# Row maxima of causal attention: rounded, split and turned by 32x32 blocks on VectorE and carried by DMA, instead of turned by TensorE and copied by ScalarE

## The reference

```python
xn = layernorm(x)
q, k, v = split(xn @ qkv_w + qkv_b, 3)          # 32 heads, D = 16
q, k = rope(q), rope(k)
scores = einsum('bqhd,bkhd->bhqk', q, k) / sqrt(D)
probs = softmax(scores + (1 - tril) * MASK_VAL)
ctx = einsum('bhqk,bkhd->bqhd', probs, v)
x = x + (ctx @ out_w + out_b) * silu(ffn(xn))
```

## Time and profile before

| | |
|---|---|
| median of 3 runs | 611.6 us (611.2 to 612.4) |
| the profiled execution's own time | 611.91 us |
| its span, first to last instruction | 610.0 us |
| TensorE busy | 590.7 us, 97% |
| VectorE busy | 383.0 us, 63% |
| ScalarE busy | 290.2 us, 48% |
| GpSimd busy | 386.2 us, 63% |
| granted TensorE clock | full in all of the span |

### The profile page before, as it was taken

One profiled execution on the slowest core, in us unless ns is written; L12 is line 12 of the kernel. 1 busy time (PEld: TensorE's weight loads), 2 busy tenths in 40 slices (PEclk: granted clock), 3 DMA queues, 4 the chain that ended last, 5 costly groups with the idle time before them and its releaser, 6 DMA issues.

```text
span 610.0 us, 9847 instructions
## 1 busy us (share of the span) xinstructions
PE 590.7 (97%) x3368; PEld 424.7 (70%) x3368; DVE 383.0 (63%) x912; ACT 290.2 (48%) x448; POOL 386.2 (63%) x598
## 2 busy tenths in 40 slices
PE   6999999999999999999999999999999999999996
PEld 5876666666677887666666666788887676767664
DVE  5986778666427489877786663366985261516257
ACT  3625777556734622276766566354122453232432
POOL 6896956656435578878575555348979594821363
PEclk9999999999999999999999999999999999999999
DMA  9788776654512237658577554942600000000002
GB/s 302 236 303 251 208 212 189 195 139 103 145 54 87 87 103 220 210 165 250 148 216 223 154 160 130 353 157 95 238 5 1 1 0 2 0 1 1 0 30 109
DMA packets 60369, 83.63 MB, mean 137 GB/s; under 512 B 17936, under 2 KB 26768, under 8 KB 60320
## 3 DMA queue, kind: packets, MB, share of 16 engines
q1 hardware_dynamic: 57968, 75.02, 41.2%
q10 hardware_dynamic: 2352, 8.00, 3.4%
HBM read 65.17 MB, written 26.99 MB: 151 GB/s over the span
## 4 chain that ended last, share of the span: by engine, by line
PE 79%; DMA 5%; DVE 3%; issue 3%; POOL 3%; ACT 3%; SPq 2%; POOLq 0%; ACTq 0%; DVEq 0%
PE proj_ps L1004 9%; PE proj_ps L1006 7%; PE proj_ps L1005 7%; PE ctx_ps L1161 5%; PE score_ps L1034 4%; PE proj_ps L1209 4%; PE proj_ps L1210 3%; PE scoreT_ps L1043 3%; PE score_ps L1004 2%; PE score_ps L1006 2%; PE score_ps L1005 2%; PE scoreT_ps L1004 2%; PE scoreT_ps L1006 2%; PE scoreT_ps L1005 2%; PE ctx_ps L1209 2%
## 5 line engine op out<-in xcount | busy, mean ns | idle before, releaser
L821 POOL TENSOR_TENSOR w_lo<-raw,w_hi 128x512 fp32r<-128x512 f32 x98 | 132.3, 1355 | 64.7 <-ACT w_hi L1374 59.2
L1555 DVE CUSTOM_DVE_ANT_0 score_ps<-score_ps,causal 128x512 f32<-128x512 f32 (+3 forms) x256 | 118.9, 522 | 60.7 <-PE score_ps L1034 60.5
L1423 ACT ACTIVATE probs_T<-scoreT_ps 128x1024 f32<-128x1024 f32 x80 | 82.2, 1027 | 46.1 <-PE scoreT_ps L1043 45.0
L1004 PE MATMUL proj_ps<-xn_hi,w_hi 128*128 128x512 f32 x224 | 96.8, 432 | 1.6 <-ACT by_sin L1352 1.2
L1006 PE MATMUL proj_ps<-xn_lo,w_hi 128*128 128x512 f32 x224 | 88.5, 395 | 0.0
L1005 PE MATMUL proj_ps<-xn_hi,w_lo 128*128 128x512 f32 x224 | 88.5, 395 | 0.0
L852 POOL TENSOR_SCALAR_AFFINE_SELECT probs_T<-probs_T 128x256 f32<-128x256 f32 x128 | 55.5, 457 | 14.2 <-ACT probs_T L1423 14.1
L1004 PEld LDWEIGHTS proj_ps<-xn_hi,w_hi 128*128 128x128 f32 x224 | 42.0, 188 | 26.6 <-issue 14.4
L1333 ACT ACTIVATE q_st<-one_turn_ps 2x512 fp32r<-2x512 f32 x64 | 37.5, 587 | 32.5 <-PE one_turn_ps L1020 32.1
L979 POOL TENSOR_TENSOR hsL<-hidden_T,hsH 128x256 fp32r<-128x256 f32 x44 | 37.6, 872 | 23.4 <-ACT hsH L1495 22.9
L1006 PEld LDWEIGHTS proj_ps<-xn_lo,w_hi 128*128 128x128 f32 x224 | 42.2, 188 | 10.0
(11 more groups left out here) (317 smaller groups left out, 1348.6 us busy)
## 6 DMA issues: line engine op xcount, KB each, us to landing
raw<-w SPq DMA_DIRECT2D x98, 256.0 KB, 2.8
rows<-rows_hi SPq DMA_DIRECT2D x32, 256.0 KB, 3.8
arranged<-tern SPq DMA_DIRECT2D x96, 85.0 KB
q_st<-rows SPq DMA_DIRECT2D x32, 200.0 KB
k_st<-rows SPq DMA_DIRECT2D x32, 200.0 KB
rows<-rows_lo SPq DMA_DIRECT2D x16, 256.0 KB, 4.3
gate_w<-arranged ACTq DMA_DIRECT2D x4, 704.0 KB, 7.2
up_w<-arranged ACTq DMA_DIRECT2D x4, 704.0 KB, 8.3
```

Source lines behind the costliest of these rows:

```text
L821: nc.gpsimd.tensor_tensor(w_lo[n % SPLIT][:, :], raw[n % RAW][:, :], F32(w_hi[n % SPLIT][:, :]), ALU.subtract).then_inc(unit_ready, 1)
L1004: nc.tensor.matmul(acc, lh, rh, start=first, stop=False)
L1423: nc.scalar.activation(probs_T[g % 2][x][:, :, :], scoreT_ps[:, :, :], ACT.Exp, scale=0.25).then_inc(probs_ready, 1)
L1555: m = nc.vector.tensor_tensor_reduce(out=block, in0=block, in1=causal[:, S - w:], scale=1.0, scalar=-3e38, op0=ALU.add, op1=ALU.max, accum ...
```

## The change

The maxima are no longer turned by TensorE. As soon as VectorE has the last maxima of a pair (slots with x = 2 and x = 4, in the same slot), it rounds them (a cast), takes the rest (a subtraction), both into `max_cols`, which is now 32 columns wide for a tile with heads and parts in columns 0 to 3, and transposes 32 x 32 blocks: four instructions, one for each quarter of the partitions, each 32 partitions x 128 numbers, into a new tile `max_rows` of 32 x 512. Rows 0 to 3 of it hold what `q_st` needs. `max_out` stays where it was in ScalarE's list, but issues two DMAs of 2 rows x 512 numbers instead of two copies. The scores_T products that use the maxima now wait for these DMAs (`max_stored`); VectorE waits for the DMAs of the pair before it overwrites `max_rows`. `join_maxima`, `max_turn`, `ident_r` and the cast that filled it are gone, the turns of the maxima leave the list of bank users, and `deal` counts nothing for them and has 215 in place of 230 in one bound, which moves single triples between neighbouring slots.

```diff
@@ -181,14 +181,14 @@
-    held = [43 * (score_in(s) is not None) + 33 * (prob_in(s) is not None) + 22 * (max_in(s) is not None) + 53 * (ctx_in(s) is not None)
+    held = [43 * (score_in(s) is not None) + 33 * (prob_in(s) is not None) + 53 * (ctx_in(s) is not None)
             + (sum((14, 86, 64, 43, 22)[kt + 1] for kt in (-1, *pv_in(s)[1])) if pv_in(s) else 0) for s in range(SCORE_SLOTS)]
         room += length - held[s]
-        while len(at) < TRIPLES and (room >= triple / 2 and at.count(s) < 3 or held[s] + triple * at.count(s) < 230):
+        while len(at) < TRIPLES and (room >= triple / 2 and at.count(s) < 3 or held[s] + triple * at.count(s) < 215):
             k = len(at)
@@ -211,8 +211,6 @@
             at["ctx", ctx_in(s)] = len(at)
-        if max_in(s) is not None:
-            at["max", max_in(s)] = len(at)
         for kc in turns_in(s):
@@ -331,13 +329,12 @@
     ident = sb("ident", [P, P], f32)
-    ident_r = sb("ident_r", [P, P], f32r)
     centre_m = sb("centre_m", [P, P], f32)
     rope_sin = sb("rope_sin", [P, S], f32)
-    at[0] += E * 4
+    max_rows = sb("max_rows", [32, S], f32)
     out_bias = sb("out_bias", [P, E], f32)
@@ -383,7 +380,7 @@
     at[0] += 30720
-    max_cols = sb("max_cols", [P, 2, NT, 34], f32r)
+    max_cols = sb("max_cols", [P, NT, 32], f32r)
     o_h = at[0]
@@ -482,7 +479,6 @@
     ident_in = sem("ident_in")
-    ident_rounded = sem("ident_rounded")
     v_used = sem("v_used")
@@ -518,6 +514,8 @@
     max_ready = sem("max_ready")
+    max_turned = sem("max_turned")
+    max_stored = sem("max_stored")
     scoreT_done = sem("scoreT_done")
@@ -829,20 +827,6 @@
-            def join_maxima(b, j):
-
-                pool.wait_ge(part_ready, TASKS * b + PARTS * (j // 2) + (3, 5)[j % 2])
-                if PAIRS * b + j == 0:
-                    pool.wait_ge(cols_set, 1)
-                if PAIRS * b + j >= 2:
-                    b0, j0 = divmod(PAIRS * b + j - 2, PAIRS)
-                    pool.wait_ge(turned, use(b0, ("max", j0)) + 1)
-                maxima = row_max[:, j % 2, :].rearrange("p (t h) -> p t h", t=NT)
-                hi, lo = (max_cols[:, j % 2, :, x:34:32] for x in range(2))
-                nc.gpsimd.tensor_scalar(hi, maxima, 1.0, 0.0, ALU.mult, ALU.add).then_inc(max_hi, 1)
-                pool.wait_ge(max_hi, PAIRS * b + j + 1)
-                nc.gpsimd.tensor_tensor(lo, maxima, F32(hi), ALU.subtract).then_inc(max_ready, 1)
-
             def keep_causal(b, s):
@@ -905,15 +889,13 @@
                     if b == 0 and u == 1:
-                        nc.gpsimd.memset(F32(max_cols[:, :, :, :]), 0.0).then_inc(cols_set, 1)
+                        nc.gpsimd.memset(F32(max_cols[:, :, :]), 0.0).then_inc(cols_set, 1)
                 if b:
                 for s in range(SCORE_SLOTS + 2):
-                    if max_in(s) is not None:
-                        join_maxima(b, max_in(s))
                     for u in split_in_slot(s):
@@ -1008,17 +990,6 @@
                 return w_hi[n % SPLIT], w_lo[n % SPLIT]
-
-            def max_turn(b, j):
-                pe.wait_ge(max_ready, PAIRS * b + j + 1)
-                if PAIRS * b + j == 0:
-                    pe.wait_ge(ident_rounded, 1)
-                n = use(b, ("max", j))
-                if TURN_BANK[n][1]:
-                    pe.wait_ge(turn_done(n), TURN_BANK[n][1])
-                for qt in range(NT):
-                    m = nc.tensor.matmul(turn_bank(n)[0:34, qt * P:(qt + 1) * P], max_cols[:, j % 2, qt, :], ident_r[:, :], start=True, stop=True)
-                m.then_inc(turned, 1)
@@ -1123,13 +1094,11 @@
                         if x in (0, 2):
-                            pe.wait_ge(*copied(b, ("max", 2 * g + x // 2)))
+                            pe.wait_ge(max_stored, 32 * (PAIRS * b + 2 * g + x // 2 + 1))
                         if s > LAG:
                     fill(b, s)
-                    if max_in(s) is not None:
-                        max_turn(b, max_in(s))
                     if context_in(s):
@@ -1327,11 +1296,10 @@
-                n, g = use(b, ("max", j)), GROUPS * b + j // 2
-                act.wait_ge(turned, n + 1)
+                n, g = PAIRS * b + j, GROUPS * b + j // 2
+                act.wait_ge(max_turned, n + 1)
                 for hh in range(2):
-                    m = nc.scalar.activation(q_st[g % 3][64 * hh:64 * hh + 2, j % 2, :], turn_bank(n)[32 * hh:32 * hh + 2, :], ACT.Copy)
-                m.then_inc(turn_done(n), 1)
+                    act.dma_start(F32(q_st[g % 3][64 * hh:64 * hh + 2, j % 2, :]), max_rows[2 * hh:2 * hh + 2, :]).then_inc(max_stored, 16)
@@ -1556,6 +1524,27 @@
+            def turn_maxima(b, j):
+
+                n = PAIRS * b + j
+                maxima = row_max[:, j % 2, :].rearrange("p (t h) -> p t h", t=NT)
+                hi, lo = (max_cols[:, :, x:4:2] for x in range(2))
+                dve.wait_ge(part_ready, TASKS * b + PARTS * (j // 2) + (3, 5)[j % 2])
+                if n == 0:
+                    dve.wait_ge(cols_set, 1)
+                else:
+                    dve.wait_ge(max_turned, n)
+                nc.vector.tensor_copy(hi, maxima).then_inc(max_hi, 1)
+                dve.wait_ge(max_hi, n + 1)
+                nc.vector.tensor_tensor(lo, maxima, F32(hi), ALU.subtract).then_inc(max_ready, 1)
+                dve.wait_ge(max_ready, n + 1)
+                if n:
+                    dve.wait_ge(max_stored, 32 * n)
+                for r in range(NT):
+
+                    m = nc.vector.transpose(max_rows[:, :].rearrange("p (t r i) -> p r t i", t=NT, r=4)[:, r], F32(max_cols[32 * r:32 * r + 32, :, :]))
+                m.then_inc(max_turned, 1)
+
             def norm_stats(k):
@@ -1665,8 +1654,6 @@
             norm_lo(0)
-            dve.wait_ge(ident_in, 16)
-            nc.vector.tensor_copy(ident_r[:, :], ident[:, :]).then_inc(ident_rounded, 1)
             for b in range(B):
@@ -1693,6 +1680,9 @@
                         row_maxima(b, s)
+                        g, x = score_in(s)
+                        if x in (2, 4):
+                            turn_maxima(b, 2 * g + x // 4)
                     if ctx_in(s - 1) is not None:
                         n = use(b, ("ctx", g))
```

## The result

The changed kernel took 637.5 us in the median (4 runs, 635.8 to 640.8), the kernel before 611.4 us (4 runs). The ratio is 1.043, 95% interval 1.038 to 1.048: 4% slower. The prediction said 608.5 us, faster, with a range up to 617; it had the wrong sign. The profiled execution has a span of 639.0 us against 610.0.

A forecast was written before the change was run, and what follows sets the result against it. TensorE, busy for 97% of the span, was taken as the bound. A gain of 11.4 us less 8.4 us of VectorE's block over both batches gave 3.0 us off, 608.5 us, range 603.5 to 617.

The forecast's parts named there:

- The gross gain: TensorE's list without the 32 turns of the maxima and their waits for ctx_rows: 11.4 us off.
- The two terms: On TensorE, 32 turns at 0.23 us, 7.4 us, and 8 waits for ctx_rows at 0.5 us, 4.0 us.
- What D costs TensorE: VectorE's block delays its later work and the next slot's maxima, for which TensorE's scores wait: 4.2 us a batch.
- D: VectorE's added block for each pair, cast, subtraction and four transposes: 1.4 us, bounds 1.2 to 1.8.
- six slots with x = 2: Room of about 1.35 us, read from slot 38, against D = 1.4: 0.1 us each, 0.6 us a batch.
- slot 9, "the worst": First transpose waits for a DMA issued late behind ScalarE's rope copies, delaying slot 10's maxima: 1.7 us a batch.
- the 1.6 of the prediction: Length of VectorE's block, in us, at which the net gain would be about zero.
- The transpose was put near its lower bound: VectorE's 32 x 128 transpose taken as 0.22 us, between bounds of 0.19 and 0.33 us.
- VectorE becomes the pace: Rival: in score slots, D at or above 1.75 us; about 3 us slower at 1.75, 619.5 us at 2.0; 18%.
- DMA landing: Landings into q_st of 1.7 to 2.8 us; with 2.0 us, slots 9 and 19 cost less and time is 606.5 us.
- the DMAs land too late everywhere: Rival: with landings of 3.9 us, scores_T waits 0.4 us for most of 28 pairs, VectorE too; 616 us; 12%.
- The deal, counted at nothing within 1 us: Placing the same number of triples, a few one slot later, changes nothing, within 1 us either way.

The follow-up runs named there:

- neither: Changed kernel without VectorE's block, without the DMAs of the maxima and without the wait for them ahead of scores_T: 600.2 us, 0.981.
- no_dma: Changed kernel without the 64 DMAs into q_st; scores_T waits for the last transpose, and transposes no longer wait for stores: 634.6 us, 1.037.
- unrounded_one: Changed kernel with maxima in one part (no cast or subtraction), two max_rows buffers, the old deal, one 128 x 128 transpose and four DMAs a pair: 637.6 us, 1.045.
- two_turns: Changed kernel with two transposes of 64 x 128 in place of four of 32 x 128, and four DMAs a pair in place of two: 636.9 us, 1.041.
- the run named deal: Changed kernel with nine projection triples of each batch moved from the tail of the phase into the score slots, by other weights: 651.8 us, 1.064.
- act_copies: Changed kernel with one 128 x 256 transpose a pair in place of four, and eight ScalarE copies into q_st in place of two DMAs: 617.3 us, 1.009.

## Why the prediction was wrong

**The gross gain was right as a sum.** 11.4 us predicted, 11.5 measured by neither. The two terms are not shown apart: the slots with x = 3 are 8.0 us shorter in neither than before (7.7 predicted), but those with x = 0 only 0.4, as the new deal puts three more triples of a batch into them, and neither has 2.4 us more of waits for `k_st`. A match to 0.1 us is partly luck.

**The step that failed: "What D costs TensorE".** The prediction counted 4.2 us a batch; the block costs 17.2 a batch. What failed in it is that it priced a few places and counted the rest as covered. It said of slots with x = 4 that no ctx_rows stand behind them and that "where no product stands there either, I count D as covered"; the runs put half of the loss there, 17.2 us in the 16 slots that follow. It gave six slots with x = 2 a cost of 0.1 us each after the model of slot 38, and in slot 38 that was right; but 38 is one of the roomiest. Of the slots that it did name, batch 0 of no_dma against neither gives: slot 9, "the worst" at 1.7 us, 0.7 (and its wait for the DMAs adds nothing: slots 9 and 10 take 7.5 us with them and without); slot 12 0.5 for 0.4; slot 24 0.8 for 0.4; slot 19 1.4 for 0.8; slot 2 3.1 for 0.15. The sum should have been made for each slot with a block and the one behind it. VectorE needs 0.54 us from the scores to its start, 1.64 for the maxima of x = 2 or 4, 1.77 for the block and 1.40 for the maxima of x = 3 or 0, 5.35 us, and 0.69 more where a product stands between. Against that stand the two slots' lengths without a block, from neither's trace:

```
slots     length, us           needed           late by   no_dma's slot is longer by
37, 38    2.69 + 2.96 = 5.65   5.35             0         0
27, 28    2.69 + 2.25 = 4.94   5.35             0.4       0.5
24, 25    2.33 + 2.93 = 5.26   5.35 + 0.69      0.8       0.8
34, 35    2.96 + 2.25 = 5.21   5.35 + 1.0       1.1       1.8
```

(In slots 34 and 35 the cast takes 1.17 us, 1.0 more than elsewhere, beside work of GpSimd.)

This rule gives the cost within 0.1 us in slots 8, 13, 18, 25, 28 and 33 of the first batch, but over the 30 slots behind a block, with each block's own length, only 20.8 of the 32.6 us. What it lacks is in two places. In slots 3, 10, 15 and 30 TensorE waits first for the feed-forward product behind the block, as told above: its triples need the bank which that product frees, and so the block delays TensorE inside the slot, not only at the next scores. The prediction named feed-forward products in VectorE's list only as something that shortens the room of the next maxima. And in slot 3 the clock falls on top. The kernel before shows this only in part: its slots with x = 3 take 2.5 to 3.2 us, and five of the eight fall to 2.25 once the turn, its wait and single triples are gone. The gain and the cost are in the same slots.

**The size of D was off too, and would not have saved it.** 1.4 us taken, bounds 1.2 to 1.8, 1.77 measured in the median. The cost of the block without DMAs, over neither:

```
block, us (median)   0     0.66   1.15   1.77
loss, us             0     5.0    16.1   34.4
```

(The falls of the clock are in it: one, three and five in the profiled executions, at 1.5 to 1.7 us each.)

Between the points D = 1.4 would have cost some 23 us, twice the gain; the break-even lies near 0.95 us, not at the 1.6 of the prediction. The transpose was put near its lower bound (0.22 us) on the slope of the row maxima and a start of 0.07 us, which no row and no run shows; it took 0.300 us, 0.31 from one start to the next. The sentence that stood beside it, of the Trainium skill (VectorE: DVE Perf Modes, The three transpose paths), gave 0.31 us for 128 x 128 in bf16: unrounded_one's transpose of that shape took 311 ns, in fp32.

**The rival was the right one and too small.** "VectorE becomes the pace" had its mechanism and its place, but a slope of 0.8 to 2.4 us for each 0.1 us of D, above D = 1.4 only; at 1.75 it gave 3 us slower. The measured slope between 1.15 and 1.77 is 3 us for 0.1, near the upper of the two, but the cost starts from far below 1.4, and its places include the wait of the triples, which the rival did not have.

**DMA landing.** As a cost of this change it is small: 3 us of the 26. But the landings of 1.7 and 2.8 us that the prediction worked with hold only where no loads go out beside the issue; for the second pairs of most groups it was 4.0 to 6.2 us, above the 3.9 of its rival. With two issues for each pair there is just room; with four there is not (20.6 us in two_turns, 30 in unrounded_one). The step to 606.5 us by a landing of 2.0 us is also too large on its own terms: between 1.7 and 2.8 us slot 9's cost moves by 1.1, so 2.0 saves it 0.3 of the 1.7 taken and slot 19 about half of that, 0.9 us over both batches and not 2. The rival that the DMAs land too late everywhere describes those two kernels, in the slots with x = 2.

**The deal, counted at nothing within 1 us,** cost 4.4 us beside the long block and nothing beside the short one: an edit that is free while TensorE is the bound is not when another engine is. **The clock** was not in the prediction, which put it at nothing: about 8 us of no_dma's 34.4 come with the waits. They are no separate cause, but a price that each idle stretch of TensorE can bring on top of its own length.

## What to carry to other kernels

Before work is put on an engine with a low busy share, tabulate for every slot of the pattern that follows it how long the slot will be after the change, less what that engine already does there, and do so for everything of that engine that TensorE needs, the release of a bank as well as the next input; one well-read slot says nothing of its neighbours, and a single buffer between two engines means that no slot pays for another. The break-even length of the block can be had from a kernel without it and one with it half as long. And when a shorter block is bought with more small DMAs, look at what is in the DMA engines at the moment of their issue, not at a landing in a quiet stretch.

## What the runs showed of the hardware

- The transpose on VectorE costs by its columns and hardly by its partitions: 32 x 128 took 300 ns, 64 x 128 305, 128 x 128 311, and 128 x 256 446. Four over 32 partitions took 1.24 us, one over 128 0.31.
- Small DMAs of 4 KB from ScalarE's queue landed 1.7 to 2.9 us after the start of the last issue where SyncE issued no loads of `q_st` and `k_st` beside them, and 4.0 to 6.2 us after it where 800 KB of them had just gone out (changed kernel; group 0's first pair, 4.7 us, is the exception).
- TensorE's clock went to 0.50 for 3.41 us (6.83 at times, as at 81.85 us in the run named deal) in kernels in which it waited in the score slots, and to full again; idle products in the waits took four of five such falls away in the profiled executions. A fall in a slot in which TensorE is busy cost 1.5 to 1.7 us (slot 21, 3.56 us without and 5.25 with it).
- Eight copies of 2 x 128 on ScalarE took 2.5 us (307 ns each, act_copies), two of 2 x 512 1.19.
